# Layer two's output: reciprocals stay on VectorE, the copy goes to ScalarE, the multiply and the combine to GpSimd

## The reference, cut to what matters

```
scores = einsum('bhqd,bhkd->bhqk', q, k) * scale        # 32 score heads of width 16
scores = where(causal, scores, lowest)
probs = softmax(scores, axis=-1)
attn_out = einsum('bhqk,bhkd->bhqd', probs, v)           # values of width 32
attn1, attn2 = attn_out[:, 0::2], attn_out[:, 1::2]
attn = attn1 - lambda_full * attn2
attn = attn * rsqrt(mean(attn * attn, axis=-1, keepdims=True) + EPS) * ln_w
```

## Time and profile before

| What | Value |
|---|---|
| median of three runs (lowest, highest) | 2314.46 us (2312.27, 2315.24) |
| the profiled execution | 2310.82 us; span from first to last instruction 2309.1 us |
| busy over the whole span | PE 97%, DVE 69%, ACT 54%, POOL 40% |
| busy in layer two's heads, 1860 to 1960 us of the span | PE 100.00, DVE 89.79, ACT 69.03, POOL 19.86 us of 100 |
| granted TensorE clock, whole span and 1860 to 1960 us | 0.983 and 1.00 of full speed |

### The profile page before, as it was taken

How to read it: one execution, slowest core, us unless ns; L and a number is a source line. 1 busy time by engine, 2 the same in 40 slices (tenths; PEclk the granted TensorE clock), 3 DMA queues, 4 the chain that set the end, 5 groups by cost and what they waited for, 6 DMA issues and landing times. The chain is left out here.

```text
span 2309.1 us, 41769 instructions
## 1 busy us (share of the span) xinstructions
PE 2232.7 (97%) x14456; PEld 1279.5 (55%) x14456; DVE 1591.8 (69%) x3637; ACT 1241.4 (54%) x2480; POOL 922.2 (40%) x761
## 2 busy tenths in 40 slices
PE   8899999999999999999999999978999999999999
PEld 6663333333333333678888888866544444444477
DVE  3346899999999996554444443453589898988677
ACT  3116778778787878531221212252367676666744
POOL 4006898888999999510000000002011121212152
PEclk9998999999999999999999999998899999999999
DMA  6754322233222100220000000004703321220001
GB/s 216 159 129 57 79 34 29 29 43 43 29 30 35 23 2 2 69 73 28 1 28 27 27 27 27 1 1 132 152 22 55 44 42 25 43 44 2 2 19 55
DMA packets 59000, 108.98 MB, mean 47 GB/s; under 512 B 12028, under 2 KB 23292, under 8 KB 58808
## 3 DMA queue, kind: packets, MB, share of 16 engines
q1 hardware_dynamic: 57960, 103.39, 21.9%
q0 software_dynamic: 848, 3.15, 0.4%
HBM read 73.75 MB, written 31.46 MB: 46 GB/s over the span
## 5 line engine op out<-in xcount | busy, mean ns | idle before, releaser
L983 DVE TENSOR_REDUCE l_maxima<-l_p_ring 128x1 f32<-128x512 f32 x1280 | 813.9, 684 | 90.8 <-PE l_p_ring L655 73.0
L900 ACT ACTIVATE l_w_hi_prob<-l_p_work 128x512 f32<-128x512 f32 (+3 forms) x1280 | 600.1, 535 | 217.8 <-PE l_p_work L680 208.9
L655 PE MATMUL l_p_ring<-xT_all 48*128 48x512 f32 (+3 forms) x1680 | 490.5, 419 | 0.0
L680 PE MATMUL l_p_work<-xT_all 50*128 50x512 f32 (+3 forms) x1680 | 471.3, 417 | 0.0
L655 PEld LDWEIGHTS l_p_ring<-xT_all 48*128 48x128 f32 x1680 | 243.5, 186 | 334.1 <-DVE l_maxima L983 204.6
L608 POOL TENSOR_TENSOR l_part<-l_w_hi_prob,l_w_hi_prob 128x1024 f32<-128x1024 f32 x128 | 304.2, 2378 | 184.7 <-ACT l_w_hi_prob L900 145.3
L622 POOL TENSOR_SCALAR_AFFINE_SELECT l_w_hi_prob<-l_w_hi_prob 128x256 f32<-128x256 f32 x256 | 105.7, 419 | 511.2 <-ACT l_w_hi_prob L900 511.2
L680 PEld LDWEIGHTS l_p_work<-xT_all 50*128 50x128 f32 x1680 | 234.8, 185 | 130.1 <-ACT l_w_hi_prob L900 85.5
L608 POOL TENSOR_TENSOR l_part<-x_prob,x_prob 128x1024 f32<-128x1024 f32 x126 | 297.3, 2382 | 23.0 <-ACT x_prob L900 19.8
L900 ACT ACTIVATE x_prob<-l_p_work 128x512 f32<-128x512 f32 x512 | 275.4, 601 | 52.0 <-PE l_p_work L680 51.8
L700 PE MATMUL l_p_work<-l_w_hi_prob,v_all 128*32 128x512 f32 (+3 forms) x1536 | 302.1, 499 | 0.3 <-ACT l_w_hi_sums L853 0.2
(11 more groups left out here) (188 smaller groups left out, 3642.3 us busy)
## 6 DMA issues: line engine op xcount, KB each, us to landing
xT_all<-q_parts SPq DMA_DIRECT2D x180, 128.0 KB
q_parts<-l_part SPq DMA_DIRECT2D x64, 256.0 KB
xT_all<-k_parts SPq DMA_DIRECT2D x90, 128.0 KB
k_parts<-l_part SPq DMA_DIRECT2D x40, 256.0 KB
xT_all<-k_parts SPq DMA_DIRECT2D x90, 64.0 KB
v_all_ffn_w<-in_L_ffn_gate_w_T SPq DMA_DIRECT2D x8, 512.0 KB, 3.6
v_all_ffn_w<-in_L_ffn_up_w_T SPq DMA_DIRECT2D x8, 512.0 KB, 4.5
v_all_ffn_w<-in_L_ffn_down_w_T SPq DMA_DIRECT2D x8, 512.0 KB, 5.7
```

The lines of the kernel that those rows point to most:

```text
L655: filling = pe.matmul(p_ring[:, L.bank_at["maxima", n, u, sub] % L.ring, 0:keys], q[i][rows, n % 2, qt * P:(qt + 1) * P], k[i][rows, L.k_h ...
L680: pe.matmul(p_score[:, at % SCORE_BANKS, off:CH], k[i][rows, L.k_head(n), kt * P:(kt + 1) * P], q[i][rows, n % 2, qc * CH + off:(qc + 1) * ...
L900: act.activation(prob[step % L.prob_ring][:, sub, off:CH], p_score[:, at % SCORE_BANKS, off:CH], ACT.Exp, scale=HD ** -0.5).then_inc(exped, 1)
L983: dve.tensor_reduce(to, scores, AX.X, ALU.max).then_inc(freed, 1)
```

## The change

VectorE's `keep` shrinks to the reciprocal. A new `copy_turned_half` on ScalarE copies the turned values of a half into `half`, which frees the ring's bank (`turn_copied`). A new `combine` on GpSimd scales the second sub-head's reciprocals by minus lambda, multiplies `half` with the reciprocals, and adds the two sub-heads into `attn`.

On ScalarE the copy of half 0 of head n stands behind the exponential of head n+1, step 0, sub-head 0 (`copied_after` 1), and that of half 1 behind head n+1, step 5, sub-head 0 (`copied_after` 11). At that second place `copy_out` of head n+1, half 0, stands too; the copies are listed by head, so the new copy comes before it. On GpSimd `combine(n, 0)` stands behind the select of head n, step 11, and `combine(n, 1)` behind step 6 of head n+1, where no select is (`COMBINED_AT`). The squaring of a finished head moves from step 6 to step 9 of the next head. Layer one keeps its order.

```diff
+COMBINED_AT = [11, 6]
...
-           20, (3, 2))
+           20, (3, 2, 1, 11))
...
+            def combine(n, qc):
+                kept = QC * n + qc
+                pool.wait_ge(out_recip, kept + 1)
+                pool.tensor_scalar(recip[:, :, 1, :], recip[:, :, 1, :], neg_lambda, None, ALU.mult).then_inc(out_kept, 1)
+                pool.wait_ge(turn_copied, kept + 1)
+                pool.wait_ge(out_kept, L.outputs * kept + 1)
+                pool.tensor_tensor(half[:, :, :, :], half[:, :, :, :], recip[:, :, :, :].to_broadcast([P, QPC, 2, VD]),
+                                   ALU.mult).then_inc(out_kept, 1)
+                pool.wait_ge(out_kept, L.outputs * kept + 2)
+                tile = (n // NH) * KT + qc * QPC
+                to = attn[:, :].rearrange("p (t c) -> p t c", c=D)[:, tile:tile + QPC, (n % NH) * VD:(n % NH + 1) * VD]
+                pool.tensor_tensor(to, half[:, :, 0, :], half[:, :, 1, :], ALU.add).then_inc(out_kept, 1)
...
+                    if not L.joint and s == COMBINED_AT[1] and n:
+                        combine(n - 1, 1)
+                    if not L.joint and s == COMBINED_AT[0]:
+                        combine(n, 0)
...
-                if older[0] == "turn" and L.joint:
+                if older[0] == "turn":
                     pe.wait_ge(turn_copied, L.freed_at[older])
...
+            def copy_turned_half(n, qc):
+                kept = QC * n + qc
+                act.wait_ge(out_recip, kept + 1)
+                if kept:
+                    act.wait_ge(out_kept, L.outputs * kept)
+                turned = p_ring[:, L.bank_at["turn", n, qc] % L.ring, :].rearrange("p (b s w) -> p b s w", b=QPC, s=2)
+                act.activation(half[:, :, :, :], turned[:, :, :, 0:VD], ACT.Copy).then_inc(turn_copied, 1)
...
-                for qc, s in enumerate(L.qc_last if not L.joint else (S - 1,) * 3):
+                for qc, s in enumerate(L.qc_last + [S - 1] * QC if not L.joint else (S - 1,) * 3):
...
-                    if not L.joint:
+                    if not L.joint and which >= QC:
+                        copy_turned_half(n, which - QC)
+                    elif not L.joint:
                         copy_out(n, which)
...
-                if at % (2 * S) == (S // 2 if L.joint else S) and at >= 2 * S * behind:
+                if at % (2 * S) == (S // 2 if L.joint else S + S // 2) and at >= 2 * S * behind:
...
                 if kept:
-                    dve.wait_ge(out_kept, kept)
+                    dve.wait_ge(out_kept, L.outputs * kept - 1)
                 dve.reciprocal(recip[:, :, :, 0], cols[:, :, :, VD]).then_inc(out_recip, 1)
-                dve.wait_ge(out_recip, kept + 1)
-                dve.tensor_tensor(half[:, :, :, :], cols[:, :, :, 0:VD], recip[:, :, :, :].to_broadcast([P, QPC, 2, VD]),
-                                  ALU.mult).then_inc(freed, 1)
-                dve.wait_ge(freed, L.freed_at["turn", n, qc])
...
-                dve.scalar_tensor_tensor(
-                    out=to, in0=half[:, :, 1, :], scalar=neg_lambda, in1=half[:, :, 0, :],
-                    op0=ALU.mult, op1=ALU.add).then_inc(out_kept, 1)
```

More of the change, by code:

```diff
@@ L107, in __init__ @@
         self.rounds = KT if self.joint else len(self.steps)
-        self.outputs = 3 if self.joint else QC
+        self.outputs = 3
         self.pairs = []
@@ L135, in __init__ @@
         for item in self.user:
-            if item[0] == "turn" and self.joint:
-                self.freed_at[item] = 2 * (item[1] + 1)
+            if item[0] == "turn":
+                self.freed_at[item] = 2 * (item[1] + 1) if self.joint else QC * item[1] + item[2] + 1
             else:
@@ L374, in attention_phase @@
         out_recip, out_kept = sem("out_recip"), sem("out_kept")
+        turn_copied = sem("turn_copied")
         if L.joint:
             paired, ones_summed, ones_copied = sem("paired"), sem("ones_summed"), sem("ones_copied")
-            turn_copied = sem("turn_copied")
         loaded, squared, averaged, wo_ready = sem("loaded"), sem("squared"), sem("averaged"), sem("wo_ready")
@@ L631, in _ @@
                 finish(HEADS - 1)
+            else:
+                combine(HEADS - 1, 1)
             mix.gpsimd(pool, lambda pool: pool.wait_ge(summed, HEADS * L.rounds))
@@ L838, in ring_free @@
             def ring_free(pe):
[L839 to L842, removed]
+                pe.wait_ge(turn_copied, 2 * HEADS)
             mix.tensor(pe, ring_free)
@@ L870, in square @@
                 rows = slice((n // NH) * KT, (n // NH + 1) * KT)
-                act.wait_ge(out_kept, L.outputs * (n + 1))
+                act.wait_ge(out_kept, L.outputs * (n + 1) * (1 if L.joint else QC))
                 if n:
@@ L1010, in keep @@
                 if kept:
-                    dve.wait_ge(out_kept, kept)
+                    dve.wait_ge(out_kept, L.outputs * kept - 1)
                 dve.reciprocal(recip[:, :, :, 0], cols[:, :, :, VD]).then_inc(out_recip, 1)
-                dve.wait_ge(out_recip, kept + 1)
-                dve.tensor_tensor(half[:, :, :, :], cols[:, :, :, 0:VD], recip[:, :, :, :].to_broadcast([P, QPC, 2, VD]),
-                                  ALU.mult).then_inc(freed, 1)
-                dve.wait_ge(freed, L.freed_at["turn", n, qc])
-                tiles = attn[:, :].rearrange("p (t c) -> p t c", c=D)
-                tile = (n // NH) * KT + qc * QPC
-                to = tiles[:, tile:tile + QPC, (n % NH) * VD:(n % NH + 1) * VD]
-                dve.scalar_tensor_tensor(
-                    out=to, in0=half[:, :, 1, :], scalar=neg_lambda, in1=half[:, :, 0, :],
-                    op0=ALU.mult, op1=ALU.add).then_inc(out_kept, 1)
             def invert(n):
```

## The result

The changed kernel takes 2335.12 us (median of four runs, 2330.79 to 2336.53) against 2313.36 us before (four runs). The ratio is 1.0096, 95% interval 1.0083 to 1.0109: slower by 0.96%. The forecast was 2334.5 us, counted from 2314.46, the median of the three runs that were there when it was made.

The account below looks back on a forecast made before the run. The prediction took PE to bound the kernel, with VectorE in step behind; 0.19 + 0.48 = 0.67 us per head over 30 heads, 20.1 us, took the median 2314.5 to 2334.5, 0.9% slower; range 2312 to 2350, likeliest case 2324 to 2348.

Parts of the forecast that it names:

- The bound: Layer two's heads: PE-bound, busy 100.00 of 100, chain all PE's but 0.2%, with VectorE in step behind it.
- The gain costed at 0: Taking L1014 and L1020, 1.55 us per head, off VectorE buys nothing, as PE does not wait for it.
- the rival: VectorE is the bound after all: 0.9 us per head faster, 28 us, 2287; chance 0.11.
- Place B: Change of heads: GpSimd's combine of half 0 delays the select and PE's next first sum, 0.48 us per head.
- The line through two durations: GpSimd's add of 256 and of 1024 columns: 2.15 ns a column, 0.18 fixed; product 0.61, add 0.46 us.
- The estimate by the Trainium skill's factor of two: GpSimd at twice VectorE's durations, 0.85 and 0.70: 0.96 us at the change of heads, 2349 in total; not adopted.
- Place A: Ahead of copy_out of half 0: ScalarE's new copy delays copy-out and bank, overlapping; PE's sum 0.19 us later per head.
- The square: Moved from step 6 to step 9, delaying the second exponential there by 0.30: cost 0, at most 0.05 per head.
- The sum: 0.19 + 0.48 = 0.67 us per head, counted for 30 heads: 20.1 us.
- the first head would lose nothing: In the first head or two PE has idle time anyway, so 30 of 31 occurrences are counted.
- The end: After the last head, before the projection's first tiles: costed at 0, between -1 and +1 us.
- What would show it: Signs: VectorE about 80, period 16.7 to 17.3 us, waits at select (about 0.5 us) and copy-out, PE below 100.00.

Follow-up runs that it names:

- both: Changed kernel with GpSimd's combine of half 0 behind the next head's first select and ScalarE's copy of half 1 behind step 3; 2314.84 us, ratio 1.0012.
- both and the square: Changed kernel with the two moves of "both" and the square of a finished head back at step 6; 2311.30 us, ratio 0.9997.
- VectorE lighter: Kernel before, with one product straight into the output in place of product and combination, second sub-head left out; 2311.17 us, ratio 0.9996.
- combine late: Changed kernel with GpSimd's combine of a head's first half behind the next head's first select instead of ahead of it; 2322.75 us, ratio 1.0044.
- copy behind: Changed kernel with the copy of half 1 one exponential later, behind copy_out instead of ahead of it; 2370.84 us, ratio 1.0253.
- VectorE heavier: Kernel before, with VectorE's product of 256 columns done twice in each half; 2323.81 us, ratio 1.0056.

## Why the prediction was right, point by point

**The bound.** PE was the bound: taking work from VectorE brought no gain in three kernels (both, both and the square, VectorE lighter). The gain costed at 0 measured 0.00 us a head. The grounds that the prediction gave, a PE busy for 100.00 and a chain that is PE's, were weaker than it took them to be: "combine late" shows both and still loses 0.36 us a head. That nothing was hidden behind VectorE is shown by the periods. The rule of the Trainium skill that the rival named (Perfetto Trace Analysis, Identifying the Most-Contended Engine) would have picked VectorE, since PE's weight loads were 44 of 100 busy (the page's other measure, MFU, was not worked out); the measurement decides against it here.

**Place B.** The mechanism and the size held: 0.48 forecast, 0.46 measured. The working counted a signal of 0.06 twice between the copy's end and the product (1831.35 to 1831.47); the trace has 0.10 there, so this did no harm. The line through two durations of other widths gave 0.61 and 0.46 us for product and add; they take 0.615 and 0.459. The estimate by the Trainium skill's factor of two (GPSIMD Engine Reference, Engine selection), 0.96 for the place, was twice too much: against VectorE's 0.424 and 0.352 the factors here are 1.45 and 1.30, and GpSimd's own rows were the better source.

**Place A was mis-sized.** Forecast 0.19, measured 0.29. The prediction had two delays of about the same length overlap, the copy-out's (0.19) and the bank's (0.18), and so put the sum 0.19 late. Both came out a little shorter, 0.17 and 0.14 counted from the head's first sum, since the copy was quicker than taken (0.378 us instead of 0.43, and the next instruction starts 0.26 after it instead of 0.30). The copy-out was off the path: 0.17 us lie between its end and the sum. The bank's delay set the place, and it cost more than its wait, for which the prediction had no term. From the start of the maxima to the sum it is 0.61 us (1826.69 to 1827.30), where it was 0.45 (1820.74 to 1821.19). In "copy behind" the same stretch takes 0.62 (1840.32 to 1840.94), though the copy-out there ended at 1839.50. Moving the copy to either side confirmed the mechanism: early, the whole 0.29 comes back; one place later it is 1.4.

**The square** was costed at 0, at most 0.05; it costs 0.07 to 0.08. The exponentials behind it are needed sooner than their sum, since they also free the score banks: the scores of step 11, sub-head 0, wait for the exponential of step 9, sub-head 1. In "both" that exponential ends at 1828.79 and the scores' weight load starts 0.05 later; in "both and the square" the exponential ends 0.27 ahead of the load, and the load comes 0.08 sooner, counted from the head's first sum. That the square is the cause is shown by the run; the wait is read from these two traces.

**The sum.** 0.82 a head, not 0.67; 25 us over 31 heads, not 20. That the first head would lose nothing, as the forecast assumed, is not shown. In the changed kernel's trace the first head starts at 1654.92 us instead of 1657.95, with nothing changed ahead of it, and the second at 1682.36 instead of 1683.12, so the first head takes 2.3 us longer. In the other kernels the first head starts between 1655.7 and 1659.8 and the second between 1682.1 and 1686.3, so how much of this belongs to the one profiled execution stays open. From the second head's start, 0.8 earlier, the next 30 heads lose 24.5, and the spans differ by 23.9; the medians differ by 21.8, and the forecast counted from 2314.46 where the four runs have 2313.36. The close agreement of 2334.5 with 2335.12 is thus in part luck of these few microseconds.

**The end** was costed at 0: from the last turn to the end of the span it is 113.26 us, before 113.41.

**What would show it.** VectorE near 80 of 100 (78.55), PE below 100.00 (98.05) and the select ahead of the first sum came as said. The period came out at 17.43 for 17.3, and the waits named the select at 0.4 us. They name the copy-out ahead of step 4's sum too, as forecast, but only for the sum's weight load (0.23 us), and the copy-out had ended 0.17 before it.

## What to carry to other kernels

Before work is moved off a busy engine, look whether the chain of work passes through that engine at all: here an engine that was busy for 90% of the time, with waits against its name, was still not worth relieving. Neither the busy share nor the chain proves this, since both hid 0.36 us a head in "combine late"; one run of a cut-down version of the old kernel does, by its period. When work moves to an idle engine, its place in that engine's queue is the price: ask what stands behind it and who waits for that, and what buffer its completion frees. Here the right places made a loss of 0.96% into no change, with the same instructions.

## What the runs showed of the hardware that had not been expected

A wait of 0.14 us on the matmul queue cost 0.29: the group of maxima and scores behind it took 0.61 instead of 0.45 us. In "copy behind" it is alike: 1.22 us of wait at the first of them, 1.40 by the third instruction. The trace shows where 0.10 of the difference lies. In the kernel before, the weights of the group's first two matmuls are loaded at 1820.51 and 1820.52, while PE is still busy with the scores, and the two matmuls start within 0.01 us of each other at 1820.74. In the changed kernel the loads wait as well; they start at 1826.69 and 1826.76, and the matmuls 0.10 apart (1826.69 and 1826.79), as in "copy behind" (1840.32 and 1840.42). That the lost head start of the loads is the reason is argued, not tested.

GpSimd's select always took 0.41 us in the changed kernel (mean 406 ns), where the one at the change of heads took 0.52 before. VectorE's combination L1020, now gone, ran from 1830.47 to 1830.82 there, beside the select from 1830.57. Between 1760 and 2160 us of the kernel before all 24 selects of over 0.5 us overlap a combination, and the other 169 take 0.41 and overlap none. In "VectorE lighter", which has no combination, and in "VectorE heavier", where it starts as the select ends (0.05 us of overlap), every select takes 0.41. The Trainium skill (SBUF — State Buffer, Who interferes with whom) says that a VectorE instruction with two SBUF inputs contends with a GpSimd instruction that reads SBUF; these runs agree. They don't show the select held for as long as the combination runs: the two overlap for 0.25 us and the select takes 0.11 longer.

VectorE's slack is one-sided: 0.96 us a head less brought 0.00, while 0.9 us a head more (a second product at 0.42 us a half, and its wait) cost 0.43, with VectorE at 92.27 and 92.11 of 100 in the two windows from 1860 to 2060 us.
